# First self attention: two steps of the softmax pipeline woven by halves, the row maximum carried through the second half's reduction

## The reference

```python
q = qkv[:, 0].reshape(b, h, s, hd).astype(jnp.bfloat16)
k = qkv[:, 1].reshape(b, h, s, hd).astype(jnp.bfloat16)
v = qkv[:, 2].reshape(b, h, s, hd).astype(jnp.bfloat16)
scale = jnp.sqrt(jnp.asarray(hd, dtype=jnp.bfloat16))
scores = jnp.einsum('bhqd,bhkd->bhqk', q, k) / scale
attn = jax.nn.softmax(scores, axis=-1)
o = jnp.einsum('bhqk,bhkd->bhqd', attn, v)
```

## Time and profile before

| | |
|---|---|
| time before, median of 3 runs | 3449.01 us (3447.76 to 3451.31) |
| span of the profiled execution | 3459.0 us (the page gives no other time for it) |
| first and last start of the reductions (L376) in it | 59.4 us and 686.3 us |
| busy over the whole span: PE, DVE, ACT, POOL | 91%, 68%, 49%, 50% |
| mean granted clock of TensorE | 0.956 of full speed |

### The profile page before, as it was taken

How to read it: one execution, slowest core, us unless ns; L and a number is a source line. 1 busy time by engine, 2 the same in 40 slices (tenths; PEclk the granted TensorE clock), 3 DMA queues, 4 the chain that set the end, 5 groups by cost and what they waited for, 6 DMA issues and landing times. The chain is left out here.

```text
span 3459.0 us, 62575 instructions
## 1 busy us (share of the span) xinstructions
PE 3138.3 (91%) x24201; PEld 1810.0 (52%) x24201; DVE 2354.6 (68%) x4987; ACT 1708.5 (49%) x2102; POOL 1731.8 (50%) x1163
## 2 busy tenths in 40 slices
PE   7999999989999999999999953958989999999797
PEld 3666666644555555555555523846654434444346
DVE  5999999945655665566656556156429978888518
ACT  3888888823434444444444441222234656666641
POOL 5999999814777777777777831322460000000012
PEclk9999999989999999999999976988997999999898
DMA  2000000020000000000000054730021111120101
GB/s 70 6 2 2 2 2 2 26 55 1 4 1 4 1 4 4 1 4 1 4 1 1 1 160 136 239 86 1 1 43 18 18 18 18 18 26 10 33 1 37
DMA packets 65530, 91.51 MB, mean 26 GB/s; under 512 B 9586, under 2 KB 55539, under 8 KB 64371
## 3 DMA queue, kind: packets, MB, share of 16 engines
q1 hardware_dynamic: 61682, 83.17, 9.5%
q0 software_dynamic: 3072, 4.34, 0.7%
q10 hardware_dynamic: 512, 0.26, 0.0%
HBM read 62.34 MB, written 10.65 MB: 21 GB/s over the span
## 5 line engine op out<-in xcount | busy, mean ns | idle before, releaser
L969 DVE TENSOR_REDUCE x0hm<-x0pM 128x1 f32<-128x400 f32 (+1 forms) x1024 | 520.8, 563 | 378.3 <-PE x0pM L871 378.2
L434 POOL TENSOR_SCALAR rows<-rows,mb 128x1024 bf16<-128x1024 bf16 x512 | 567.5, 1119 | 98.1 <-DVE mb L382 98.1
L376 DVE TENSOR_SCALAR_CACHE_REDUCE rows<-pS 128x1024 bf16<-128x1024 f32 x512 | 605.8, 1209 | 2.0 <-PE pS L312 1.5
L445 ACT ACTIVATE prT<-pP 128x1024 bf16<-128x1024 bf16 x512 | 521.9, 1024 | 110.1 <-PE pP L323 92.6
L1433 DVE TENSOR_REDUCE x1hm<-x1pM 128x1 f32<-128x400 f32 (+1 forms) x1024 | 519.1, 567 | 67.4 <-PE x1pM L1319 64.2
L1552 ACT ACTIVATE x1pr<-x1pST 128x1024 f32<-128x1024 f32 (+1 forms) x416 | 403.8, 1022 | 216.1 <-PE x1pST L1371 216.0
L831 POOL TENSOR_TENSOR x0acc<-x0acc,x0pr 128x1024 f32<-128x1024 f32 (+1 forms) x176 | 422.1, 2398 | 110.2 <-ACT x0pr L1080 95.0
L831 POOL TENSOR_TENSOR x0acc<-x0acc,o_nat 128x1024 f32<-128x1024 f32 (+1 forms) x176 | 419.1, 2381 | 72.3 <-ACT o_nat L1080 53.5
L1080 ACT ACTIVATE x0pr<-x0pST 128x1024 f32<-128x1024 f32 (+1 forms) x208 | 212.9, 1024 | 279.6 <-PE x0pST L915 279.6
L1080 ACT ACTIVATE o_nat<-x0pST 128x1024 f32<-128x1024 f32 (+1 forms) x208 | 213.0, 1024 | 278.4 <-PE x0pST L915 278.0
L2666 POOL MEMSET f_tri<- 128x128 f32 x1 | 0.2, 209 | 675.7 <-POOLq L1224 675.7
(11 more groups left out here) (367 smaller groups left out, 5125.2 us busy)
## 6 DMA issues: line engine op xcount, KB each, us to landing
m_w<-in_moe_w1T SPq DMA_DIRECT2D x16, 1024.0 KB
m_w<-in_moe_w2T SPq DMA_DIRECT2D x16, 1024.0 KB, 9.1
acc_d<-m_zero SPq DMA_DIRECT2D x8, 514.0 KB, 9.5
m_acc<-acc_d SPq DMA_DIRECT2D x8, 514.0 KB, 5.6
x1sq<-x1qh SPq DMA_DIRECT2D x32, 128.0 KB, 4.0
x1sk<-x1kh SPq DMA_DIRECT2D x32, 100.1 KB, 3.6
rows_d<-m_xr SPq DMA_DIRECT2D x1, 2176.0 KB, 9.0
g_xN<-in_x SPq DMA_DIRECT2D x1, 2048.0 KB
```

The source lines that it names most:

```text
L376: nc.vector.tensor_scalar(rows[u][:, half * 1024:(half + 1) * 1024], pS[half][:, :], 1.0, None, ALU.mult, ALU.max, accum_out=mx[u][:, half ...
L434: nc.gpsimd.tensor_scalar(r, r, -1.0, mb[u][:, 0:1], ALU.mult, ALU.add).then_inc(s_df, 1)
L445: nc.scalar.activation(prT[u][:, half * 8:(half + 1) * 8, :], pP[half][:, :, :], ACT.Exp, scale=-1.0 / HD ** 0.5).then_inc(s_ex, 1)
L969: emptied(nc.vector.tensor_reduce(hm[g % 2][:, a, t, i % 8 // 2:i % 8 // 2 + 1], bank(name)[:, 0:w], AX.X, ALU.max, negate=True), name)
```

## The change

- **Order on DVE.** The steps are taken in pairs, n even with n + 1. The four halves of a pair are reduced in the order (n, 0), (n + 1, 0), (n, 1), (n + 1, 1). The new function `turn(n, u, half)` gives the place of a half in this order: 2n + 2 half for an even step, 2n - 1 + 2 half for an odd one. `s_rd` and `s_sc` count turns.
- **The maximum.** The first half's maximum goes to `mx[u]`, now one column. The second half's `tensor_scalar` has `mx[u]` as its second scalar operand, which is the initial value of the reduction, and writes the maximum of the whole row into `mb[u]`. It waits for the first half's maximum, which was written two turns before. `maximum` (L382) and its semaphore are gone.
- **PSUM.** Step n uses `pS[n % 2]` for both of its halves, so the two buffers still alternate from turn to turn.
- **POOL** waits for the turn of the step's second half instead of `maximum`.
- **PE.** `step(n, u)` now issues, in front of the transposes of (n, 0) and (n, 1), the scores of turns 2n + 4 and 2n + 5 (before, of turns 2n + 6 and 2n + 7). Ahead of the loop it issues the scores of two steps instead of three.
- **The outputs** of 8 steps are normalized one step earlier, in a pair that begins at k % 8 == 4: `sums` after the first turn of the pair, `recip` after the second, `quotients` after the third.

```diff
--- before.py
+++ after.py
@@ -262,7 +262,7 @@
             NU = 4
             rows = [m2.sb(f"rows{i}", [P, T], BF16) for i in range(NU)]
             prT = [m2.sb(f"prT{i}", [P, 16, P], BF16) for i in range(NU)]
-            mx = [m2.sb(f"mx{i}", [P, 2], BF16) for i in range(NU)]
+            mx = [m2.sb(f"mx{i}", [P, 1], BF16) for i in range(NU)]
             mb = [m2.sb(f"mb{i}", [P, 1]) for i in range(NU)]
             sb_ = [m2.sb(f"sums{i}", [P, 8], BF16) for i in range(2)]
             rs = [m2.sb(f"rs{i}", [P, 8]) for i in range(2)]
@@ -272,9 +272,13 @@
             pO = [b[:, 0:8 * (HD + 1)].rearrange("p (a d) -> p a d", a=8) for b in pOV]
             pV = pOV[0][:, 256:256 + D]
             s_vt = m.sem("a_vtile")
-            s_sc, s_rd, s_mx = m.sem("a_scores"), m.sem("a_rounded"), m.sem("a_max")
+            s_sc, s_rd = m.sem("a_scores"), m.sem("a_rounded")
             s_go, s_df, s_tp, s_ex = m.sem("a_begun"), m.sem("a_diff"), m.sem("a_transposed"), m.sem("a_exp")
             s_o, s_sum, s_rc, s_oc = m.sem("a_out"), m.sem("a_sum"), m.sem("a_recip"), m.sem("a_outcopied")
+            def turn(n, u, half):
+                return 2 * n - u % 2 + 2 * half
 
             def run(eng, step):
 
@@ -305,11 +309,11 @@
 
                         if n == 64 and half == 0:
                             pe_.wait_ge(s_rest, 48 * 16)
-                        if n >= 1:
-                            pe_.wait_ge(s_rd, 2 * (n - 1) + half + 1)
+                        if turn(n, n, half) >= 2:
+                            pe_.wait_ge(s_rd, turn(n, n, half) - 1)
                         for a in range(2):
                             rows_a = slice(64 * a, 64 * a + 64)
-                            mm = nc.tensor.matmul(pS[half][:, a * 512:(a + 1) * 512], qT[rows_a, n % 16, head(n)],
+                            mm = nc.tensor.matmul(pS[n % 2][:, a * 512:(a + 1) * 512], qT[rows_a, n % 16, head(n)],
                                                   kT[rows_a, 4 * half:4 * half + 4, head(n)], start=True, stop=True)
                         mm.then_inc(s_sc, 1)
 
@@ -348,8 +352,8 @@
 
                     def step(n, u):
                         for half in range(2):
-                            if n + 3 < NS:
-                                scores(n + 3, half)
+                            if n + 2 < NS:
+                                scores(n + 2 - n % 2 + half, n % 2)
                             transposes(n, u, half)
                             if n >= 2:
                                 values(n - 2, (u - 2) % NU, half)
@@ -358,9 +362,9 @@
                     pe_.wait_ge(s_first, 32 * 16)
                     pe_.wait_ge(s_firstk, 16 * 16)
                     pe_.wait_ge(s_va, 1)
-                    for n in range(3):
-                        scores(n, 0)
-                        scores(n, 1)
+                    for half in range(2):
+                        scores(0, half)
+                        scores(1, half)
                     for n in range(NS):
                         step(n, n % NU)
                     for n in (NS - 2, NS - 1):
@@ -371,15 +375,16 @@
                 def _(dve):
                     def rounded(n, u, half):
 
-                        wait(dve, s_tp, 2 * (n - NU) + 2, n - NU)
-                        dve.wait_ge(s_sc, 2 * n + half + 1)
-                        nc.vector.tensor_scalar(rows[u][:, half * 1024:(half + 1) * 1024], pS[half][:, :],
-                                                1.0, None, ALU.mult, ALU.max,
-                                                accum_out=mx[u][:, half:half + 1]).then_inc(s_rd, 1)
-                    def maximum(n, u):
-                        dve.wait_ge(s_rd, 2 * n + 2)
-                        nc.vector.tensor_tensor(mb[u][:, :], mx[u][:, 0:1], mx[u][:, 1:2], ALU.max).then_inc(s_mx, 1)
+                        dve.wait_ge(s_sc, turn(n, u, half) + 1)
+                        here = rows[u][:, half * 1024:(half + 1) * 1024]
+                        if half == 0:
+                            wait(dve, s_tp, 2 * (n - NU) + 2, n - NU)
+                            nc.vector.tensor_scalar(here, pS[u % 2][:, :], 1.0, None, ALU.mult, ALU.max,
+                                                    accum_out=mx[u][:, :]).then_inc(s_rd, 1)
+                        else:
+                            dve.wait_ge(s_rd, turn(n, u, 0) + 1)
+                            nc.vector.tensor_scalar(here, pS[u % 2][:, :], 1.0, mx[u][:, :], ALU.mult, ALU.max,
+                                                    accum_out=mb[u][:, :]).then_inc(s_rd, 1)
 
                     def sums(n, b):
 
@@ -397,37 +402,34 @@
                                                 rs[b][:, :].unsqueeze(2).to_broadcast([P, 8, HD]), ALU.mult)\
                             .then_inc(s_oc, 8)
 
-                    def step(n, k):
-                        u = k % NU
-                        first = isinstance(n, int) and n == 0
-                        outputs = k % 8 == 5 and (not isinstance(n, int) or n >= 13)
-                        b = (k - 13) % 16 // 8
+                    def pair(n, k):
+                        u, v = k % NU, k % NU + 1
+                        outputs = k % 8 == 4 and (not isinstance(n, int) or n >= 12)
+                        b = (k - 12) % 16 // 8
+                        rounded(n, u, 0)
                         if outputs:
-                            sums(n - 13, b)
-                        rounded(n, u, 0)
-                        if not first:
-                            maximum(n - 1, (u - 1) % NU)
+                            sums(n - 12, b)
+                        rounded(n + 1, v, 0)
                         if outputs:
-                            recip(n - 13, b)
+                            recip(n - 12, b)
                         rounded(n, u, 1)
                         if outputs:
-                            quotients(n - 13, b)
-                    for n in range(16):
-                        step(n, n)
+                            quotients(n - 12, b)
+                        rounded(n + 1, v, 1)
+                    for n in range(0, 16, 2):
+                        pair(n, n)
                     with dve.Fori(1, NS // 16) as h:
-                        for k in range(16):
-                            step(h * 16 + k, k)
-                    maximum(NS - 1, NU - 1)
+                        for k in range(0, 16, 2):
+                            pair(h * 16 + k, k)
                     for part in (sums, recip, quotients):
                         part(NS - 8, 1)
 
                 @block.gpsimd
                 def _(pool):
                     def step(n, u):
-                        pool.wait_ge(s_mx, n + 1)
+                        pool.wait_ge(s_rd, turn(n, u, 1) + 1)
                         pool.sem_inc(s_go, 1)
                         for half in range(2):
                             r = rows[u][:, half * 1024:(half + 1) * 1024]
```

## The result

The changed kernel is slower: 3478.32 us in the median of 4 runs (3476.2 to 3484.33), against 3450.16 for the kernel before. The ratio is 1.0075, with a 95% interval of 1.0057 to 1.0093, some 26 us (the two medians differ by 28). The profiled execution took 3477.03 us, with a span of 3475.3. Its first reduction starts at 58.9 us and the last at 708.4, where before it was 59.4 and 686.3: the loop alone is 22.6 us longer. That is most of the difference. The two profiled spans differ by only 16.3 us (3459.0 and 3475.3): outside the loop the profiled execution of before took 6 us more than that of the changed kernel, and its span lies above the times of its runs (3447.76 to 3455.74).

What follows compares the result with a forecast made beforehand. It took a knot of POOL and `maximum` to bound the old loop, a latency chain the new: 628.5 + 3.8 (`recip`) + 7.5 (value tile) = 639.8 us, 12.5 more than before, about 3462 us; range 3443 to 3484.

Steps and rivals of the forecast that it cites:

- my own chain: The main forecast for the changed kernel: about 3462 us, range 3456 to 3470, chance 0.5.
- the chain: Accumulator read through POOL, transposes, values and scores to DVE's reduction: 2.62, plus 2.29 for two turns, 4.91 us a pair.
- the operand: Scalar initial value in the second half's reduction on DVE: taken as 0 extra, upper bound 0.07 us.
- the second wait: DVE's wait for the ring of rows, now after the scores' wait in a first half: 0, upper bound 0.06 us.
- one of my own signs of being wrong: The prediction was to fail if the initial value made DVE's reduction longer than 1.21 us.
- The longer-chain rival: Upper bounds of the operand (0.07) and the second wait (0.06) both count: 17 us more, 3479; chance 0.2.
- The outputs: On DVE, `sums` and `quotients` cost nothing while it stands still; `recip` costs 0.12 us, 32 times, 3.8 us.
- The value tile: PE's extra 0.76 us in front of scores of turn 2m + 7: 0.5 lost, 15 times, 7.5 us.
- The knot of the kernel before: `maximum` on DVE held until POOL ends, POOL starting 0.21 us later: 2.43 us a step.
- DVE as the bound: Rival: DVE never stands still, a pair takes 4.58 us, 31 us less, 3418; chance 0.05.
- POOL did not answer faster on the read: Rival: POOL starts 0.13 us behind the read instead of 0.28, pair 4.76, 3443; chance 0.25 of an early enough start.

Runs made afterwards that it cites:

- The first experiment: Changed kernel with PE issuing its scores one turn further ahead of the transposes: 3443.49 us, ratio 0.9964 to the kernel before.
- the fourth experiment: Kernel before with PE's scores two steps ahead of the transposes instead of three, order and maximum unchanged: 3488.62 us, ratio 1.0091.

## Why the prediction was right, and where its sizes were off

The direction and the mechanism held, and the time lay in the range of 3443 to 3484, near its upper end. The narrow range of my own chain, 3456 to 3470, missed it. The loop was forecast at 639.8 us and took 649.5; the difference to before was forecast as 12.5 us and was 22.6 in the profiles, some 26 by the ratio of the runs, twice the forecast. The sizes below add up to the 10 us that were missing: 0.08 a pair on the chain (of it 0.06 for the operand) are 10, the second wait adds 2, and `recip` gives 2 back.

- **The chain.** Each link came as taken: read to POOL 0.29 (0.28), POOL's first part to the transposes 1.17 (1.12 + 0.05), transposes to values 0.41, values to scores 0.33, scores to the reduction 0.44 (0.43), the first reduction 1.15. The first experiment removed the chain from PE's queue and with it the loss. The fourth made it in the old order. This cause is shown from both sides.
- **The term that was mis-sized: "So 0" for the operand.** It costs 0.06 in each second half (1274 ns against 1213), one of which lies on each pair's chain: 4.99 instead of 4.93, 8 us in 128 pairs. I had it as the upper bound of a rival and had preferred the row of 256 elements with 142 ns of fixed time. The better row was the other one, of the same kind of instruction, 1.28 for 1024 elements with such an operand: it has the 0.07 more. A longer reduction was also one of my own signs of being wrong, and that sign came true. The longer-chain rival's reason was therefore half right. That the time of 3478 lies beside its 3479 is in part luck: its other half, 0.06 a pair for the second wait, did not come, and the loops explain 22.6 us of the difference only.
- **The second wait.** "I take 0": on the plain steps that holds (0.44), but once in a head it was 0.13, over my upper bound of 0.06, and 2 us in all.
- **The outputs.** `sums` and `quotients` cost nothing, as forecast. `recip` cost 0.07 instead of 0.12 (pairs of 5.06 against 4.99): the reduction behind it is 0.05 shorter, 1.23 instead of 1.28. That has nothing to do with the operand. Without it the row is 1.17 instead of 1.22 and the pair 5.00 instead of 4.93, and the 1.17 stood already in the kernel before, where I overlooked it.
- **The value tile.** 0.48 a head against 0.5, in the place and by the wait that was named.
- **The knot of the kernel before.** The explanation of the 2.43, `maximum` held by POOL, is supported by the reduction over two columns: nothing else was changed, and the hold is gone in every row (143 to 156 ns). The row of 1.04 us in the fourth experiment, which ends with POOL's instruction, shows the hold directly. That it is not merely a shorter kind of instruction is seen in the kernel before itself, where the tensor_tensor takes 0.15 as well when POOL is not in its way. The form with a scalar operand could not tell, since it put the operand's price in the hold's place.
- **The rivals.** DVE as the bound did not come, but it is what the first experiment made of it (4.70 a pair). POOL did not answer faster on the read (0.29).

What stays open: that the 0.21 of the wait on DVE's own last instruction comes from the waiting instruction in between was only read in the records; no run took that instruction away. In the last step of the kernel before, `maximum` started 0.11 behind the read with no waiting instruction between. Of the 26 us by the runs, the loop explains 22.6; the rest is within the interval.

## What to carry to other kernels

When a hand-written order is changed on one engine, look at how far ahead the next engine's feeding work stands in its queue: scores that could have run were queued behind transposes that could not. Moving them by one place turned a loss of 26 us into a gain of 12. And before an instruction is removed, ask why it takes as long as it does: half of this one's cost was a hold by another engine, and another form of the same instruction gained as much as the rewritten loop with its scores one turn further ahead (ratios 0.9965 and 0.9964).

## What the runs showed of the hardware that I had not expected

- A scalar operand read from SBUF cost 0.06 us in both sizes seen here: the reduction of 1024 elements took 1274 ns with it and 1213 without, and the join of one element 0.21 as a tensor_scalar with such an operand against 0.149 as a tensor_reduce without (these two differ in the kind of instruction as well). Behind `recip` the reduction's row was 0.05 shorter with the operand (1.23) and without it (1.17).
- The Trainium skill (SBUF — State Buffer, Who interferes with whom) has it that a Vector instruction with two SBUF inputs excludes a GpSimd instruction that reads SBUF. These runs agree. With two inputs the row of the kernel before took 201 ns in the mean, and all 223 rows that began while POOL worked ended with POOL's instruction; in the fourth experiment one lasted 1.04 us. With one input it took 149 ns (143 to 156).
- POOL starts a next step without any gap if its wait is already over: four instructions of 1.12 in 4.41.
- A register or waiting instruction of DVE that ran only once late scores had come put off the reduction behind it: by 0.13 us for the one (0.57 against 0.44), by 0.10 for the other (0.53 against 0.43).
- A value tile of four fp32 matmuls in front of bf16 transposes holds their start back longer than its weight loads last: they began at 139.72, 0.97 behind the tile's start, where the loads took 0.73 and the tile's matmuls, by their modelled ends, 1.13.
